# Flamingo block, gated cross attention and experts: other step lists for the first batch

## The reference, cut to what matters

```python
def _L0_xattn_ref(q, kv, Wq, Wk, Wv, Wo, bo):
    qh = (q @ Wq)...   # (b, 16, 512, 64)
    kh = (kv @ Wk)...
    vh = (kv @ Wv)...
    attn = softmax(einsum('bhnd,bhmd->bhnm', qh, kh) * 64 ** -0.5)
    return einsum('bhnm,bhmd->bhnd', attn, vh)... @ Wo + bo

def _L0_ffn_ref(x, gate_w, expert_w, expert_b):
    probs = softmax(x @ gate_w.T)
    comb = ...         # the two largest of 8, the others 0
    return sum(comb[e] * (x @ expert_w[e].T + expert_b[e]) for e in range(8))

x = x + tanh(g_xattn) * _L0_xattn_ref(layernorm(x), ctx, Wq, Wk, Wv, Wo, bo)
x = x + tanh(g_ffn) * _L0_ffn_ref(layernorm(x), gate_w, expert_w, expert_b)
```

## Time and profile before

| | us |
|---|---|
| time, median of 3 runs (945.22 to 947.59) | 946.51 |
| the profiled execution's own time | 948.67 |
| its span, first to last instruction | 946.9 |
| PE busy | 902.7 (95%) |
| DVE busy | 852.6 (90%) |
| ACT busy | 743.8 (79%) |
| POOL busy | 646.3 (68%) |
| mean granted TensorE clock | 0.987 of full |

### The profile page before, as it was taken

One profiled execution on the slowest core, in us unless ns is written; L12 is line 12 of the kernel. 1 busy time (PEld: TensorE's weight loads), 2 busy tenths in 40 slices (PEclk: granted clock), 3 DMA queues, 4 the chain that ended last, 5 costly groups with the idle time before them and its releaser, 6 DMA issues.

```text
span 946.9 us, 28867 instructions
## 1 busy us (share of the span) xinstructions
PE 902.7 (95%) x11376; PEld 605.1 (64%) x11376; DVE 852.6 (90%) x1853; ACT 743.8 (79%) x1093; POOL 646.3 (68%) x449
## 2 busy tenths in 40 slices
PE   6788799999999999999999999999999999999997
PEld 4245455777657776677657776577655776667873
DVE  6899799998999989999899989999899998999768
ACT  3898899778995879958896879958899588988510
POOL 4677768677695867768586776958687686877400
PEclk9899899999999999999999999999999999999999
DMA  6699899999999999989999999989999799999900
GB/s 222 143 179 167 146 161 190 165 150 165 171 193 149 158 148 197 183 141 157 180 180 160 153 162 189 186 146 157 150 187 187 137 154 171 169 169 164 143 24 23
DMA packets 549142, 150.97 MB, mean 159 GB/s; under 512 B 537592, under 2 KB 547216, under 8 KB 548752
## 3 DMA queue, kind: packets, MB, share of 16 engines
q1 hardware_dynamic: 549008, 149.13, 94.7%
HBM read 11.70 MB, written 4.19 MB: 17 GB/s over the span
## 4 chain that ended last, share of the span: by engine, by line
PE 47%; DVE 25%; ACT 12%; issue 8%; DMA 3%; POOL 3%; SPq 1%; ACTq 0%; DVEq 0%; POOLq 0%
PE MB L1338 24%; PE ST L1480 9%; PE PV L1502 9%; DVE nmax L1021 8%; ACT pf L832 5%; ACT p_s L842 4%; PE MB L1350 3%; DMA pt_s<-p_s 3%; POOL p_s L654 2%; DVE acc L956 2%; DVE QL L1001 2%; DVE x L924 1%; DVE o_n L1044 1%; DVE v_s L1012 1%; ACT v_s L758 1%
## 5 line engine op out<-in xcount | busy, mean ns | idle before, releaser
L654 POOL TENSOR_TENSOR p_s<-pf,p_s 128x1024 f16<-128x1024 f32 x254 | 542.1, 2136 | 217.3 <-ACT p_s L842 169.1
L832 ACT ACTIVATE pf<-ST,shifts 128x512 f32<-128x512 f32 x512 | 324.4, 691 | 92.2 <-DVE shifts L1027 89.9
L1021 DVE TENSOR_REDUCE nmax<-ST 128x2 f32<-128x1024 f32 x256 | 310.4, 1217 | 17.6 <-PE ST L1480 15.8
L842 ACT ACTIVATE p_s<-pf 128x1024 f16<-128x1024 f32 x254 | 270.7, 1069 | 3.2
L1502 PEld LDWEIGHTS PV<-v_s,pt_s 128*128 128x128 f16 x6096 | 204.3, 98 | 43.6 <-issue 27.5
L1502 PE MATMUL PV<-v_s,pt_s 128*128 128x65 f16 x6096 | 215.7, 193 | 4.7 <-DVE o_n L1044 2.7
L1338 PE MATMUL MB<-ex_s,x2t_s 128*128 128x256 f16 (+1 forms) x1380 | 166.8, 276 | 1.1 <-DVE x L924 1.0
L1338 PEld LDWEIGHTS MB<-ex_s,x2t_s 128*128 128x128 f16 x1380 | 131.7, 98 | 23.6 <-DVE x L924 2.3
L1480 PE MATMUL ST<-KH,QH 64*128 64x512 f16 x512 | 100.8, 390 | 16.3 <-ACT pf L832 14.0
L975 DVE SCALAR_TENSOR_TENSOR acc<-MB,m,acc 128x256 f32<-128x256 f32 x224 | 95.6, 476 | 4.4 <-PE MB L1338 3.6
L1480 PE MATMUL ST<-KH,QL 64*128 64x512 f16 x512 | 99.0, 383 | 0.0
(11 more groups left out here) (174 smaller groups left out, 986.5 us busy)
## 6 DMA issues: line engine op xcount, KB each, us to landing
pt_s<-p_s SPq DMA_TRANSPOSE x508, 3.4
xin<-x SPq DMA_DIRECT2D x7, 512.0 KB, 4.9
out<-acc SPq DMA_DIRECT2D x7, 512.0 KB, 3.9
kvin<-kv_t SPq DMA_DIRECT2D x8, 256.0 KB, 4.4
stage_e<-expert_t SPq DMA_DIRECT2D x1, 2048.0 KB, 11.1
stage_o<-wo SPq DMA_DIRECT2D x1, 1024.0 KB, 5.8
stage_q<-wq SPq DMA_DIRECT2D x1, 768.0 KB, 7.3
xin<-x SPq DMA_DIRECT2D x2, 256.0 KB, 2.9
```

The costliest lines, as they stand in the source:

```text
L654: pool.tensor_tensor(p_s[:, slot, 1, :, :], pf[:, it.ring(p, u, PF_SLOTS), :, :], p_s[:, slot, 0, :, :], ALU.subtract).then_inc(p_lo, 1)
L832: last = act.activation(pf[:, (n - 1) % PF_SLOTS, i, :], ST[u % 2][:, i, :], ACT.Exp, bias=shifts[:, u % 2, i:i + 1])
L842: act.activation(p_s[:, it.ring(p, u, P_SLOTS), 0, :, :], pf[:, it.ring(p, u, PF_SLOTS), :, :], ACT.Copy).then_inc(p_hi, 1)
L1021: dve.tensor_reduce(nmax[:, t % 2, :, 0], ST[t % 2][:, :, :], AX.X, ALU.max, negate=True)\
```

## The change

In each of the four tables the list of FIRST is replaced. Counted word by word, the new list of every engine has the same words the same number of times, so that no instruction is added or removed. The lists of LOOP and LAST, the numbers `VALUES_BACK`, `LOW_BACK` and the like, and all functions stay. Since jobs are given their banks in the order of PE's list, the bank of a job of FIRST can change. The diff:

```diff
--- before.py
+++ after.py
@@ -68,13 +68,14 @@
 
 PE_ORDER = {
     FIRST: (
-        "scores", "scores pj q2", "scores v0,0 v3,0 values", "scores v1,0 values", "scores",
-        "scores values values v2,0 k2", "scores values q3", "scores q4", "scores values values values",
-        "scores v0,1 values", "scores k3 k4 values", "scores k5", "scores q5", "scores values values lsum ot0 v1,1",
-        "scores", "scores values values v3,1", "scores values values", "scores q6 ot1 values values", "scores v2,1",
-        "scores values k7 values k6", "scores values values", "scores wo0,0 values bound", "scores wo0,1 values ot3",
-        "scores q7 ot2", "scores values values", "scores xt1 values xt0 wo1,1", "scores values", "scores wo1,0 k1",
-        "scores values values q0", "scores values ot4 ot5 values", "scores k0", "scores q1 wo2,0 wo2,1",
+        "scores", "scores pj", "scores v1,0 values values values v3,0", "scores v2,0 v0,0 values",
+        "scores values q2 values", "scores k2 k3 values", "scores values q3", "scores", "scores v0,1", "scores v1,1 k4",
+        "scores values values q4", "scores values values ot0 v2,1", "scores values lsum", "scores v3,1 values", "scores",
+        "scores values values values bound values", "scores k5", "scores values values q5 ot1", "scores q6",
+        "scores wo0,0 values", "scores wo0,1", "scores k6 k7", "scores values q7", "scores ot3 values",
+        "scores ot2 values xt1", "scores values values xt0", "scores values values",
+        "scores wo1,1 values values wo1,0 ot4", "scores", "scores values ot5 q0 k0", "scores values k1",
+        "scores q1 wo2,0 wo2,1",
     ),
     LOOP: (
         "scores", "scores v3,0 values v2,0 values", "scores", "scores ot6 values values q2 values values",
@@ -103,11 +104,11 @@
 
 ACT_ORDER = {
     FIRST: (
-        "exp", "exp ph copy hi hi hi copy", "exp hi copy", "exp copy", "exp hi copy", "exp hi copy", "exp hi copy",
-        "exp hi copy", "exp hi copy", "exp hi copy", "exp hi copy", "exp hi copy", "exp hi copy", "exp lh copy lh",
-        "exp lh copy hi", "exp lh hi copy hi", "exp hi copy", "exp hi lh copy", "exp lh hi copy", "exp hi copy hi",
-        "exp context copy lh", "exp lh hi copy", "exp hi hi copy", "exp lh copy lg", "exp hi copy", "exp hi lh copy",
-        "exp lh copy", "exp lh hi copy hi", "exp hi copy hi", "exp hi copy", "exp hi copy", "exp copy",
+        "exp", "exp ph copy hi hi hi copy", "exp hi copy", "exp hi copy", "exp hi copy", "exp hi copy", "exp hi copy",
+        "exp hi copy", "exp hi copy hi", "exp copy", "exp hi copy hi", "exp hi copy", "exp hi copy lh",
+        "exp lh copy lh lh", "exp lh copy", "exp lh lh hi lh copy", "exp hi copy", "exp hi copy", "exp hi copy lh",
+        "exp lg copy", "exp hi copy hi", "exp hi copy", "exp hi copy", "exp hi copy", "exp hi copy", "exp lh copy hi",
+        "exp context copy lh", "exp hi lh copy", "exp hi hi copy hi", "exp hi copy", "exp hi copy", "exp copy",
     ),
     LOOP: (
         "exp", "exp copy hi hi hi copy", "exp hi copy", "exp hi copy hi", "exp hi copy", "exp hi copy", "exp copy",
@@ -127,17 +128,17 @@
 
 DVE_ORDER = {
     FIRST: (
-        "maximum shift rq", "maximum shift pt", "maximum take shift", "maximum normalise take take shift",
-        "maximum lm shift lm normalise", "maximum take shift", "maximum lm shift take take",
-        "maximum bound normalise shift lm", "maximum normalise shift", "maximum take take shift",
-        "maximum take shift lm take", "maximum normalise shift", "maximum take lm shift",
-        "maximum take shift normalise ls", "maximum take shift", "maximum normalise sums1 shift",
-        "maximum ll moments1 take normalise shift take", "maximum ll shift take take normalise", "maximum take shift",
-        "maximum ll shift normalise ll", "maximum take normalise take shift", "maximum take ll shift take",
-        "maximum take take shift", "maximum take ll normalise shift", "maximum take ll shift take normalise",
-        "maximum ll shift take ll", "maximum take shift", "maximum normalise shift take ll take",
-        "maximum normalise take shift ll", "maximum take take shift", "maximum normalise take gp shift",
-        "maximum take shift ll take take take",
+        "maximum shift rq", "maximum shift pt", "maximum take shift", "maximum take shift take", "maximum lm shift take",
+        "maximum take shift lm", "maximum normalise take shift lm", "maximum take shift lm",
+        "maximum normalise take shift bound", "maximum normalise normalise shift take",
+        "maximum take take normalise shift lm", "maximum normalise shift lm", "maximum take shift",
+        "maximum ls normalise shift sums1", "maximum",
+        "maximum shift take shift moments1 normalise ll take take take normalise", "maximum",
+        "maximum shift take ll shift ll ll", "maximum take shift take normalise", "maximum ll shift take",
+        "maximum take shift ll", "maximum take shift", "maximum take shift take normalise", "maximum ll shift take",
+        "maximum normalise take shift", "maximum take normalise shift ll take", "maximum normalise shift gp",
+        "maximum take shift take ll normalise take", "maximum take shift ll ll", "maximum take shift",
+        "maximum take take shift take", "maximum ll shift normalise take take take",
     ),
     LOOP: (
         "maximum shift", "maximum shift normalise", "maximum take shift take normalise",
@@ -171,9 +172,9 @@
 
 POOL_ORDER = {
     FIRST: (
-        "residual low", "low", "low", "low", "low", "low", "low", "low", "low", "low", "low", "low", "low", "low", "low",
-        "low", "power1 low", "low", "low", "low", "low", "norm1 low", "low", "low", "low", "context low", "low",
-        "scale low", "low", "low", "low", "low",
+        "low", "residual low", "low", "low", "low", "low", "low", "low", "low", "low", "low", "low", "low", "low", "low",
+        "power1 low", "norm1 low", "low", "low", "low", "scale low", "low", "low", "low", "low", "low", "low", "low",
+        "context low", "low", "low", "low",
     ),
     LOOP: (
         "low", "low", "low", "low", "low", "low", "low", "low", "low", "power2 low", "norm2 low", "residual low", "low",
```

## The result

The changed kernel takes 950.94 us, the median of four runs from 949.29 to 951.35, against 946.36 for the kernel before. The ratio is 1.0049 with a 95% interval of 1.0033 to 1.0066. It is 4.6 us slower where I had forecast 2.6 us faster.

A forecast was written before the change was run, and what follows sets the result against it. The first batch was taken as bound by DVE's work plus its waits, later ones by PE. Terms of +1.07 - 0.83 + 0.5 - 3.39 - 1.18 + 1.2 = -2.63 us gave 943.9, own range 941.5 to 946.2, 8-in-10 range 940.3 to 947.8.

The forecast's parts named there:

- third high part at the start: ACT's row 1: v2,0 behind scores 3 delays the exponential; waits of 2.07 and 0.6 replace 0.90 + 0.71, +1.07 us.
- late scales: `lm` and `lsum` each move one row earlier, to rows 11 and 12; DVE's waits of 0.54 and 0.29 go, -0.83 us.
- statistics wait for x: `sums1`, moved from row 15 to 13, waits for SP's load of x; +0.5 us, bounds 0 and +1.5.
- `context` before c_mul: Bound taken in row 15 and context in row 26 remove DVE's wait at 101.09; -3.39 us.
- wo1,1 before scores 26: PE's wo1,1 moves to row 27, removing DVE's wait at 114.87; -1.18 us.
- the term for the collisions: Line 1213's twelve DVE low parts meeting POOL's: excess 6.6 us in place of 5.4, +1.2 us; bounds 0 and 11.8.
- the cover in rows 22 to 29: PE's scores 23 ready only 0.1 us before DVE wants them; new waits 0 to 1.5 us, 0 likeliest.
- My layout: New lists laid out row by row with steps from the timelines; second batch's opening maximum near 131.7 against 133.88.
- the collisions as a rival at 0.12: POOL's low part comes between new `ll ll` pairs in DVE's rows 17 and 28; excess 14.1 us, up to 951.4; chance 0.12.
- its own sign: Line 1213 taking over 18 us would show the collisions rival right; 15.5 us over its twelve was expected.
- the later batches swallowed: Rival: PE held at the second batch's entry by something unmoved, so the gain ends there; 946.5, chance 0.13.
- The clock: Rival: three more half-rate PE stretches at critical scores cost 2.0 us; 945.9, chance 0.07.

The follow-up runs named there:

- after_ll17: Changed kernel with two of the three `ll` of DVE's row 17 moved to row 15, the third to the row's end; 945.86 us, ratio 1.0008.
- after_nc: Changed kernel with DVE's 12 late-weight low parts replaced by one-input reductions, POOL writing zeros in the prologue; 947.31 us, ratio 1.0011.
- after_gp: Changed kernel with `gp`, the gate's low parts, moved from DVE's row 26 to row 22 between two takes; 948.18 us, ratio 1.0030.
- ctx_ll: Kernel before with `context` in ACT's row 23 and `ll` of DVE's rows 16, 17 and 19 moved inside their rows; 940.80 us, ratio 0.9959.
- after_v20: Changed kernel with the third `hi` of ACT's row 1, for v2,0, moved to row 2 behind the exponential; 950.87 us, ratio 1.0051.
- before_ctx: Kernel before with one word moved: `context` from ACT's row 20 to row 23; 940.76 us, ratio 0.9945.
- before_nc: Kernel before with DVE's 12 late-weight low parts replaced by one-input reductions, POOL writing zeros in the prologue; 948.58 us, ratio 1.0033.
- four repairs: Changed kernel with row 17's `ll` spread, `gp` in row 22, ACT's third high part behind the exponential, `sums1` in row 14; 943.88 us, ratio 0.9987.
- before_pile: Kernel before with `ll` of DVE's row 16 and the first of row 19 moved into row 17, making three there; 946.09 us against 945.92.

## Why the prediction was wrong

I had read the bound rightly: the first batch was DVE's work plus DVE's waits, the later batches passed the change on whole (109.67 and 109.71 us), and the sum was to be made of these two. Step by step, for the first batch of the profiled executions:

| term | forecast | measured |
|---|---|---|
| third high part at the start | +1.07 | +1.12 |
| late scales | -0.83 | -0.83 |
| statistics wait for x | +0.5 | +1.33 |
| `context` before c_mul | -3.39 | -3.39 |
| wo1,1 before scores 26 | -1.18 | -1.18 |
| new waits in rows 15 to 20 | 0 | +3.1 |
| DVE's busy time | +1.2 | +4.2 |
| sum | -2.6 | +4.4 |

The four terms that took a wait of the trace and asked what the lists do with it came out to a tenth. For the three that take a wait away this is the mechanism. For the first it is in part luck: I had 2.07 and 0.6 in rows 4 and 5, and the same words gave 2.73 us of waits in the changed kernel, but 1.65 in after_ll17, 2.99 in after_nc and 3.07 in after_gp. The wait for x was mis-sized by 0.8, inside its bounds of 0 and 1.5. SP issued the load 42.5 us after the batch's first maximum in place of 41.8, and it took 5.1 us in place of 4.9; in after_gp this wait was 0.77. Two steps failed.

The first is the term for the collisions. For the twelve low parts alone I had +1.2 and they cost +2.1. But I had asked only about line 1213, as the one in which the trace of before showed the excess. The gate's bias, also an instruction with two SBUF inputs, took 0.47 us there because it lay free, and it didn't enter the sum; it cost +1.95. That is no accident of one execution: in the four kernels that have `gp` in row 26 behind the moved lists it took 2.38 to 2.42, in the eight others 0.47. The query weights and the late scales moved by +0.65 and -0.78, but these two differ as much between executions with the same words (2.45 us in the kernel before and 3.05 in ctx_ll, 1.78 and 0.17). Gaps and smaller ones make up the rest. The bounds should have had every instruction of that form, not the ones that had collided.

The second is the sentence that the cover in rows 22 to 29 is thin, 0 to 1.5 us, of which I take 0. The waits came, but in rows 16 to 20. My layout had put 0.7 us of excess on row 17 and two free low parts behind it, where they took 2.38, 0.74 and 2.61. Behind them PE waited for the take of ot1 until 90.78, and the layout's 131.7 for the maximum that opens the second batch became 136.50. after_ll17 shows that 3.0 of these 3.1 us, as well as 2.9 of the busy time, go with two words. Of the 3.1 the collisions made the 1.35 before maximum 20, which is gone in after_nc too. The rest came before the three low parts ran, so they can't have caused it: the new lists leave DVE waiting for scores there, with nothing to fill the time. These waits are the changed kernel's and not the execution's: after_gp and after_v20 had 3.3 and 4.2 in the same rows.

I had listed the collisions as a rival at 0.12, with the mechanism as it happened in row 17: POOL's queued low part comes in beside a pair, and the second pays. Its 951.4 is near the measured 950.94 by luck. It wanted 14.1 us of excess in the twelve and by its own sign over 18 us for them; they had 7.5 and 16.4. The pair in row 28 took 1.75 and 0.74, without POOL in between. The rival's price counted only the late low parts and left out the gate's bias and who stands behind them all.

By the Trainium skill, "SBUF — State Buffer", section "Who interferes with whom", an instruction of VectorE with two SBUF inputs and one of GpSimd that reads SBUF shut each other out to the end, and issue order decides who is held up. The traces agree on both sides: 2.61 us against 0.74 for DVE, 2.38 against 2.13 for POOL, and 0.68 at most for the reduction with one input. The rule was in my text as support for a rival. It should have carried the term, since it names the gate's instruction as much as the late weights.

Of the other rivals: the later batches swallowed nothing. The clock did not add, as the mean granted clock of the first batch is 0.91 in both kernels, and what a half-rate stretch costs wasn't tried by itself. In the faster variants it rose with the gain: 0.94 in before_ctx, 0.95 in after_ll17 and after_nc, 0.97 in before_nc. How much of their gain came by way of PE's faster clock isn't separated. What the order on PE is worth apart from DVE's is also left open. after_nc and before_nc have it at 1.3 us lower by their times, which is not clear of their intervals, and at 1.1 us higher by one first batch each.

## What to carry to other kernels

When lists are reordered, a wait can be priced from the trace of before, but an instruction's duration can not, if it depends on what another engine does beside it. Before summing, mark every instruction that can collide, whether or not it did, price each at its longest with whatever is queued behind it, and treat a layout by hand as void from the first place where such a pair meets. And look first for a wait that one word cures: `context` behind its scale was worth 5.8 us by itself, more than the new lists gave even with four repairs (1.3).

## What the runs showed of the hardware that I had not expected

An instruction over 8 partitions and 256 columns, 0.47 us when free, took 2.42 us beside a low part of POOL. One over 3 columns (late_div, a TENSOR_SCALAR with a single SBUF input) took 1.78 us in the kernel before and 1.00 in the changed one, and both times ended within 0.02 us of POOL's instruction. In before_nc, before_pile and ctx_ll, with POOL idle beside it, it took 0.17. The 24 reductions with one input were never lengthened. The load of x took 4.2 to 5.1 us to land in the traces of the first batch, and with DVE 3.1 us earlier at the statistics it landed only 1.9 earlier (after_v20).
